# The mask of two heads out of four multiplied into the exponentials on GpSimd, in a gated cross-attention program on one core

## The reference

```python
x = x + tanh(g_xattn[0]) * xattn0(layernorm(x), ctx)        # part 1: 16 heads of width 64, no mask
x = x + tanh(g_ffn[0])   * ffn0(layernorm(x))               # part 2: self-attention, then 8 experts
x = x + tanh(g_xattn[1]) * xattn1(ctx, ctx, layernorm(x), mask)   # part 3: 16 heads of width 16, masked
x = x + tanh(g_ffn[1])   * ffn1(layernorm(x))               # part 4: self-attention and 8 experts
# part 3, for each head, 512 queries against 1601 keys:
energy = einsum('nqhd,nkhd->nhqk', q, k)
energy = where(mask == 0, -1e20, energy)
attn = softmax(energy / sqrt(256), axis=3)
out = einsum('nhql,nlhd->nqhd', attn, v).reshape(...) @ w_out.T + b_out
```

## Time and profile before

| | us |
|---|---|
| median of 3 runs | 4080.57 |
| the three runs | 4080.57, 4083.59, 4043.93 |
| the profiled execution | 4040.12 |
| its span, first to last instruction | 4038.2 |

### The profile page before, as it was taken

How to read it: one execution, slowest core, us unless ns; L and a number is a source line. 1 busy time by engine, 2 the same in 40 slices (tenths; PEclk the granted TensorE clock), 3 DMA queues, 4 the chain that set the end, 5 groups by cost and what they waited for, 6 DMA issues and landing times.

```text
span 4038.2 us, 44140 instructions
## 1 busy us (share of the span) xinstructions
PE 3513.2 (87%) x18248; PEld 1466.0 (36%) x18248; DVE 1990.7 (49%) x3277; ACT 1433.0 (35%) x1639; POOL 997.5 (25%) x481
## 2 busy tenths in 40 slices
PE   8999999989999899996639379889897989798976
PEld 4443444444344344442227112242234222422252
DVE  3445555454565465553410465455645564555334
ACT  3333444433443344432312024414441445143513
POOL 3555543554453554453000300000000000000000
PEclk9999999999999999997769679989898999898988
DMA  3000000010000000000044100100010000100000
GB/s 137 11 11 29 10 7 11 10 38 7 11 6 31 16 7 11 11 9 25 1 130 132 55 30 17 35 19 17 17 34 26 17 17 22 37 17 17 16 11 6
DMA packets 64783, 108.29 MB, mean 27 GB/s; under 512 B 4461, under 2 KB 49157, under 8 KB 63046
## 3 DMA queue, kind: packets, MB, share of 16 engines
q1 hardware_dynamic: 61510, 97.08, 7.5%
q0 software_dynamic: 3072, 8.39, 0.7%
HBM read 88.68 MB, written 16.78 MB: 26 GB/s over the span
## 4 chain that ended last, share of the span: by engine, by line
PE 79%; DVE 10%; ACT 4%; POOL 3%; issue 2%; another core or an unknown queue 2%; DMA 1%; DVEq 0%; ACTq 0%; SPq 0%; POOLq 0%
PE ring L1179 9%; PE pv L1073 9%; PE ring L1058 9%; PE pv L1200 8%; PE ring L1141 4%; DVE slim L1577 3%; PE ring L1185 3%; PE ring L1042 3%; PE ring L1173 3%; PE ring L1019 2%; PE ring L1033 2%; PE ring L1034 2%; PE ring L1020 2%; PE ring L1062 2%; PE ring L1258 2%
## 5 line engine op out<-in xcount | busy, mean ns | idle before, releaser
L1442 POOL TENSOR_TENSOR wide<-wide 124x1024 f32<-124x1024 f32 (+1 forms) x352 | 828.0, 2352 | 227.0 <-ACT wide L1341 216.2
L1348 ACT ACTIVATE wide<-ring 124x1024 f32<-124x1024 f32 (+2 forms) x544 | 527.4, 1021 | 528.6 <-PE ring L1179 528.6
L1577 DVE CUSTOM_DVE_ANT_0 slim<-ring,slim 128x802 bf16<-128x802 f32 x512 | 508.3, 993 | 351.1 <-PE ring L1141 329.6
L1341 ACT ACTIVATE wide<-ring 124x1024 f32<-124x1024 f32 (+1 forms) x416 | 425.9, 1026 | 615.5 <-PE ring L1062 580.4
L1561 DVE TENSOR_REDUCE max_a<-ring 128x2 f32<-128x802 f32 x512 | 508.1, 995 | 216.9 <-PE ring L1042 216.4
L1073 PE MATMUL pv<-wide 124*64 124x512 f32 (+1 forms) x1664 | 452.3, 623 | 34.6 <-ACT wide L1341 34.6
L1058 PE MATMUL ring<-wide 64*124 64x512 f32 (+1 forms) x1664 | 445.9, 614 | 1.1 <-ACT slim L1348 1.1
L1587 DVE TENSOR_REDUCE slim<-ring 128x2 f32<-128x1024 f32 x256 | 310.8, 1224 | 167.7 <-PE ring L1153 163.9
L1456 POOL CAST slim<-slim 128x1601 bf16<-128x1601 f32 x16 | 24.4, 1528 | 1385.2 <-PE ring L1141 927.7
L1141 PE MATMUL ring<-slim 32*128 32x401 bf16 x1024 | 274.9, 371 | 88.7 <-DVE max_b L1577 58.2
L1179 PE MATMUL ring<-slim 32*124 32x512 f32 (+2 forms) x2176 | 323.4, 664 | 22.6 <-DVE slim L1602 8.8
(11 more groups left out here) (233 smaller groups left out, 4127.9 us busy)
## 6 DMA issues: line engine op xcount, KB each, us to landing
slim<-in_ctx_k SPq DMA_DIRECT2D x16, 800.5 KB, 4.5
wide<-in_w_pair SPq DMA_DIRECT2D x32, 384.0 KB, 3.2
slim<-in_ctx_v SPq DMA_DIRECT2D x16, 744.0 KB
wide<-in_w SPq DMA_DIRECT2D x16, 512.0 KB, 5.8
wide<-in_we SPq DMA_DIRECT2D x8, 1024.0 KB, 5.9
wide<-in_ctxT SPq DMA_DIRECT2D x4, 1601.0 KB, 6.9
wide<-padded_x SPq DMA_DIRECT2D x8, 640.0 KB, 7.2
expert_rows<-wide SPq DMA_DIRECT2D x8, 640.0 KB, 3.8
```

What stands on the lines that cost most here:

```text
L1341: sc.activation(exps_a[0:kn, slot_of[unit], :], slot[0:kn, :], ACT.Exp, scale=WIDE ** -0.5).then_inc(scalar_done, 1)
L1348: sc.activation((exps_2 if blk == 2 else exps_34)[0:kn, first + 2 * i:first + 2 * i + 2, :].rearrange("p h n -> p (h n)"), ring_t[0:kn, ba ...
L1442: po.tensor_tensor(sums[0:kn, :], sums[0:kn, :], view, ALU.add).then_inc(pool_done, 1)
L1577: ve.tensor_tensor_reduce(out=max_junk.rearrange("p (j n) -> p j n", j=2), in0=two[:, :, 0:CHUNK], in1=maskQ_sb[:, q, c0:c0 + 2 * CHUNK].r ...
```

## The change

1. **Mask of heads 0 and 1.** Line 1173's two products per tile go. Instead GpSimd takes the exponentials of these two heads once ScalarE has written them, cuts them at 3e38 (`tensor_scalar` with `min`, 124 x 1024 fp32) and multiplies them in place by `maskT_sb`, which now holds 1 (seen) or 0 (`tensor_tensor`). The values' product waits for GpSimd's second instruction too. Heads 2 and 3 keep their two products, now with the constant `veil_b` (125 rows) that turns 1 and 0 into 0 and -2^67.
2. **Second slot in mid-tile.** TensorE waits for the second ring slot ahead of head 2's scores and no longer ahead of head 0's, in all three parts that use `scoreb`.
3. **Expert weights.** `load_we` brings two experts (512 KB) at a time, four times per batch, into the halves of `we_sb` by turns.
4. **Masks' preparation.** By rows first, then by keys, with more steps on VectorE: fully masked queries are found (`shown`, `open_rows`), their rows are opened in both masks (four products with `ones_b` on TensorE), and the normalised queries of such rows are set to zero. The first `cast_k` moves ahead of the gathers on GpSimd.
5. **Planner.** New costs and leads: `scoreb` of part 3 costs TensorE 1.48 and not 1.95, and adds 2.6 on GpSimd; `SLACK` is 0.4 in parts 3 and 4; the maxima go by half, then head.

```diff
-MADE_3 = 0.75
-MADE_4 = -0.2
-USED_4 = -0.6
-EXPERTS_4 = -0.9
+MADE_3 = 1.1
+MADE_4 = 0.0
+USED_4 = -0.9
+EXPERTS_4 = -0.2
...
-                yield Step(1.95 if blk == 3 else 1.0, (("sc", 1.02), ("sc", 1.02)), 2, (("rowb", blk, b, g),), unit,
-                           early=0.43 if blk == 3 else 0.0)
+                yield Step(1.48 if blk == 3 else 1.05, (("sc", 1.02), ("sc", 1.02)) + ((("po", 2.6),) if blk == 3 else ()), 2,
+                           (("rowb", blk, b, g),), unit, gap=0.3, early=0.43 if blk == 3 else 0.0)
...
-        emit(on(("mask_keys_in",), *slim_done))
-        yield Step(use=(("ve", 4.0),), name=("mask_keys",), late=15.0)
-        unit = emit(("mask_keys",))
-        emit(on(("mask_rows_in",), ("vector", unit)))
-        yield Step(use=(("ve", 4.0),), needs=(unit,), name=("mask_rows",))
+        emit(on(("mask_rows_in",), *slim_done))
+        yield Step(use=(("ve", 25.0),), name=("mask_rows",), late=15.0)
         unit = emit(("mask_rows",))
+        emit(on(("mask_keys_in",), ("vector", unit)))
+        yield Step(0.4, (("ve", 16.0),), 1, (unit,), ("mask_keys",), late=6.0)
+        unit = emit(in_slot(("mask_keys",), "vector"))
...
+        yield Step(use=(("po", 4.0),), needs=(unit,), name=("cast_k", 0, 0), late=6.0)
+        emit(on(("cast_k", 0, 0), *free["b3"]))
...
-                sp.dma_start(we_sb, t["we"][:, 4 * j:4 * j + 4]).then_inc(done_sem, 16)
+                first, own = 2 * (j % 4), 2 * (j % 2)
+                sp.dma_start(we_sb[:, own:own + 2], t["we"][:, first:first + 2]).then_inc(done_sem, 16)
...
-                    if blk == 3:
-                        past.wait_ge(*at("vector", "mask_rows"))
-                        for h in range(2):
-                            pe.matmul(head_bank(unit, h)[0:kn, :], ident_b[0:kn, 0:kn], maskT_sb[0:kn, k, :],
-                                      start=True, stop=False)
-                    for lane, other in plan.second_free[unit]:
-                        past.wait_ge(*at(lane, *other))
                     for h in range(GROUP):
                         own = slice(PAD * h, PAD * h + PAD)
+                        if h == 2:
+                            for lane, other in plan.second_free[unit]:
+                                past.wait_ge(*at(lane, *other))
                         last = pe.matmul(head_bank(unit, h)[0:kn, :], keys_place(blk, g)[own, k0:k0 + kn],
-                                         queries_place(blk, g)[own, :], start=blk != 3 or h >= 2, stop=blk != 3 or h < 2)
+                                         queries_place(blk, g)[own, :], start=True, stop=blk != 3 or h < 2)
...
                     past.wait_ge(*at("scalar", "scoreb", blk, b, g, k))
+                    if blk == 3:
+                        past.wait_ge(*at("pool", "scoreb", blk, b, g, k))
...
+                elif kind == "scoreb":
+                    blk, b, g, k = a
+                    kn, first = tiles_of(blk)[k][1], exps_first(unit)
+                    past.wait_ge(pool_done, alone)
+                    past.wait_ge(*at("vector", "mask_keys"))
+                    past.wait_ge(scalar_done, plan.begin["scalar", unit] + 1)
+                    two = exps_34[0:kn, first:first + 2, :]
+                    po.tensor_scalar(two, two, FINITE, None, ALU.min).then_inc(pool_done, 1)
+                    past.wait_ge(pool_done, plan.begin["pool", unit] + 1)
+                    po.tensor_tensor(two, two, maskT_sb[0:kn, k, :].unsqueeze(1).to_broadcast([kn, 2, S]),
+                                     ALU.mult).then_inc(pool_done, 1)
```

More of the change, by code:

```diff
@@ L171, in start @@
         if step.slots:
-            at = max(at, sorted(self.ring)[step.slots - 1])
+            at = max(at, sorted(self.ring)[0], sorted(self.ring)[step.slots - 1] - step.gap)
         return at
@@ L225, in weave @@
         first = max(min(at for at, s in ready), pace.pe)
[L226 removed]
+        min((s for at, s in ready if at <= first + slack), key=Stream.progress).take(pace)
 COUNTS = {
[L231 to L232 removed]
+    "setup": (0, 1, 3, 11),
+    "mask_rows": (0, 0, 12, 0), "mask_keys": (1, 0, 5, 0),
     "ln": (0, 1, 14, 0), "turn": (1, 1, 0, 0),
@@ L1225, in _ @@
                         last = pe.matmul(place, xnT[:, 1, q * P:(q + 1) * P], weights[:, 1, :], start=False, stop=True)
+                    last.then_inc(tensor_done, 1)
+                elif kind == "mask_keys":
+                    past.wait_ge(*at("vector", "mask_rows"))
+                    for q in range(QT):
+                        last = pe.matmul(slot[:, q * P:(q + 1) * P], ones_b[:, :], shown_rows[:, q, :], start=True, stop=True)
                     last.then_inc(tensor_done, 1)
```

105 lines of the change are left out of this document (70 added, 35 removed).

## The result

The changed kernel takes 4090.9 us (median of 20 runs), the kernel before 4061.6 us (20 runs on the same chip); the ratio is 1.0065, with a 95% interval of 1.005 to 1.008. Two of the 20 runs of the changed kernel were slow ones, 4944 and 11813 us; they are in its median and not in the ratio. So it is slower by 0.65%, less than the 1% that counts as a difference here. The forecast was 3925 us with a range of 3845 to 4020: 166 us too low, and the result outside the range. The profiled execution took 4084.3 us, with a span of 4082.3 us against 4038.2.

A forecast was written before the change was run, and what follows sets the result against it. Dense tiles of the masked attention were taken as bound by TensorE. 4040 - 119 + 12 + 10 - 25 - 20 - 11 + 25 = 3912 us, raised for the median to 3925 us; range 3845 to 4020 us.

The forecast's parts named there:

- order with the planner's numbers: Masked attention: maxima no longer stand alone at a group's end; half of 54 us of waits, -25 us, between 0 and -55.
- wait in mid-tile: Second ring slot awaited ahead of head 2, not head 0: 0 us, between -10 and +10.
- masks' preparation: Experts' stage: tokens about 12 us later, sixth expert's weights held 13; together +25 us, between 0 and +40.
- first cast: GpSimd's cast, moved ahead of 32 gathers, no longer delays the first maximum by 12.53 us: -11 us.
- +10 for VectorE: VectorE instructions slowed beside GpSimd: 0 to 195 us of VectorE time, mostly hidden, so +10 us.
- the whole pair: GpSimd's cut 0.98 plus multiplication 2.35 plus handovers, 3.6 us, fits TensorE's 3.74 us tile; +12 us from some 25 tiles.
- rival A: GpSimd becomes the bound: pair and tile 5.0 us, 265 us more, 4177 us; chance 0.07.
- A's point of decision: GpSimd pair's price from which the change gains nothing: 4.35 us; 1% slower from 4.55.
- The products removed: Two mask products per tile leave TensorE: 208 tiles x 0.57 us, all counted, -119 us.
- rival B: VectorE instructions with two SBUF inputs blocked by GpSimd, 130 of 195 us on the path: about 4035 us; chance 0.10.
- The expert weights: Loads a pair of experts ahead remove TensorE's 20.5 us wait for the weights' second half: -20 us.
- Rival C: Freed time turns into other waits (ring slots, GpSimd's latency); -119 and -25 fall away, 4044 us; chance 0.12.

The follow-up runs named there:

- e13: Kernel before with the new order alone: slack, leads, maxima by chunk then head, and the planner's numbers; loads, wait and masks as before: 3939.2 us, ratio 0.968.
- e10: Kernel before with all of the change but the masks: four loads, mid-tile wait, new order, planner's numbers; both masks by products: 3914.0 us, ratio 0.963.
- e2: Changed kernel with the mask of heads 0 and 1 added by products again, nothing left on GpSimd for it: 3945.8 us, ratio 0.971.
- e1: Changed kernel without the cut at 3e38, only the multiplication left on GpSimd: 3875.4 us, ratio 0.954.
- e12: e1 with SyncE's queue rearranged: mask by keys loaded behind later experts' tokens, first keys and values behind later up-weights: 3841.0 us, ratio 0.944.
- e11: Changed kernel with the cut done by VectorE in place, only the multiplication on GpSimd: 3939.1 us, ratio 0.969.
- e4: Changed kernel plus eight GpSimd instructions in sequence on 124 x 1024 fp32 at its start; one run, read for its rows alone.

## Why the prediction was wrong

With before at 4065 us (its medians in the sets of runs were 4061.6 to 4072.6), the ratios give what each part is worth in turn. Each row is the difference of two kernels measured beside different runs of before, so it holds to 10 to 25 us:

| part, in this order | measured us | forecast us | from |
|---|---|---|---|
| order with the planner's numbers | -130 | -25 | e13 |
| loads in four, wait in mid-tile | -22 | -20 | e10 |
| masks' preparation, first cast | +35 | +14 | e2 |
| two heads' mask by one multiplication on GpSimd | -71 | -119, and +10 for VectorE | e1 |
| the cut on GpSimd | +214 | +12 (the whole pair) | changed kernel |
| sum | +26 | -128 | |

**The step that failed** is in the part on GpSimd's pair: "The cut at 3e38 has one input: I take 0.98, the upper bound is again 2.35." It takes 2.77 us. The count of inputs was taken for the price, and the cast's row for a row of the same kind. The pair is 4.95 us from start to start, not 3.6: in tiles that stand close GpSimd is the bound, which is rival A's mechanism. That the sum meets rival A's 5.0 us is luck in part: the cut is 0.42 us dearer than A had it, the multiplication 0.23 cheaper, and the handovers cost next to nothing. A's point of decision, 4.35 us, was passed, and its sign, values that wait for GpSimd, is there: 148.0 us over 208 tiles, 0.7 us each, where a tenth of a us was to show the forecast wrong. A's chance of 0.07 was far too small for a price of which the text itself says that it has no row.

The Trainium skill (GPSIMD Engine Reference, Elementwise: side-by-side cycle accounting) spoke against my 0.98 us, and I went by the cast's row. But its figure was low too: its 1.8 cycles per element are an estimate of 1.5 us for the cut, where the trace has 2.77. The sum with it, near 4000, is 91 us below the result. For two inputs its 2.6 cycles per element, an estimate of 2.2 us at the 1.2 GHz it gives GpSimd, agree with the 2.0 to 2.3 us measured.

**A second term was mis-sized, with the other sign:** the order, -130 us and not -25. I had counted only the two waits of the earlier trace rows: one fell by 13.4 us, the other stayed whole. The waits that went are spread over several lines, and the products ran faster beside them. Between the two profiled spans, 98.4 us apart, TensorE's idle time is 70.1 us less in e13, and its busy time 28.3 us less for the same products (3484.9 against 3513.2), at a mean clock of 0.924 against 0.913. The other 30 us or so of the 130 do not show in these two profiles: the profiled execution of before was shorter than any of its runs measured beside e13, and those had clocks of 0.903 to 0.907. The order is also most of why rival A's mechanism did not give rival A's 4177 us, which is 137 over the 4040 of before, where 26 was measured: 105 us of the 111 between them are the order, and the other terms nearly cancel.

**The products removed** gave 71 us, not 119. The working was right for each tile; what it left out is that the products that stay ran at a lower granted clock (0.90 against 0.93 in the stage), which is some 40 us. That the clock fell because of the missing products is not shown: e1 also has GpSimd at work for 466 us of its stage and e2 for 22, and no run varied one without the other.

**What held.** The multiplication was taken at 2.35 us and has 2.12. VectorE was hardly hurt: its busy time is 7 us more in the changed kernel than in e2 (2050.8 against 2044.1), and line 1730 has its old median and a maximum of 1447 ns. So rival B did not occur, and its term of 10 us was too large. The wait in mid-tile is worth about 13 us (4 to 23), at the edge of the forecast's 0 within 10. The expert weights gave 31 (21 to 42), a little over the forecast's 20. The first cast's 12.53 us went. The tokens' wait grew by 12.55 us, forecast 12, and the weights' by 16.84, forecast 13. In medians this part is +35 with the first cast, forecast +14, and 25 us of it lie ahead of the first maximum (2281.8 us in e10, 2306.5 in e2); the other ten are within the noise. The 13 us added to the forecast for the median were near: the median of before over 20 runs is 21.5 us above its profiled execution.

Two sums of the prediction need a word. Rival C's 4044 us needs the +12 to fall away too; with only the two terms it names the sum is 3912 + 119 + 25 = 4056 us. And rival A counted each of the 208 tiles as close to the next, where TensorE's values waited for GpSimd in 116 places.

## What to carry to other kernels

Price an instruction on another engine by a row of the very same operation with the same kinds of operands; where there is none, let the range and the rival's chance say so, and measure it by itself (eight instructions in one run settled it here). When work moves to a second engine, add up all its instructions per tile and compare with the tile's period. Beyond the period the second engine holds up the first in every tile that stands close to the next (4.95 us against 3.74 here). Below it the work can still cost: with the cut on VectorE all of it fitted, and a place behind other work in the queue kept 64 us. And measure a bundle's parts one at a time: this one held 223 us of gains (order, loads, wait, multiplication) and 249 us of losses (cut, masks' preparation), and looked like no change at all.

The fastest kernel in these runs is e12, 3841 us. It leaves the cut out, so an exponential that overflows at a masked position would not be masked. Of the kernels without that gap the fastest is e10, 3914 us, with both masks by products, 150 us below the kernel before. e11 (3939 us) keeps the cut as well; it was not run with e12's queue.

## What the runs showed of the hardware

- GpSimd on 124 x 1024 fp32 in SBUF (e4): copy 1.03 us, two tensors 2.34 us, tensor and constant 2.77 us whichever of minimum, maximum, product or sum it is. With a repeated bf16 second input two tensors take 2.00 us, and 2.12 us in the masked stage of the changed kernel.
- The same minimum takes VectorE 0.71 us (e11).
- With GpSimd busy for 1035 us of the masked stage and not 22, VectorE's same 3296 instructions took 2050.8 us and not 2044.1 (changed kernel and e2).
- TensorE's mean granted clock in the masked stage was 0.93 in e2, 0.91 in the kernel before, 0.90 in e1 and 0.85 in the changed kernel, where TensorE waited 148 us for GpSimd. From e1 to the changed kernel, for the same 17836 products, that was 68 us of busy time, a third of what the cut cost. What sets it is not shown: TensorE is busy for 89% of the stage before and for 92% in e1, whose clock is no higher.
